# DLRM tower on one core: the order of the step turned, the pairwise products two samples wide, the flattened product in six slots

## The reference, cut to what matters

```
e = stack([tbl_f[ids[:, f]] for f in range(26)])        # 2048 x 26 x 64
x = layer_norm(dense @ Wd.T)                            # 128 per sample
y = layer_norm(e @ Ws.T); y = einsum('bne,pn->bep', y, Wsi); y = layer_norm(y)
T = concatenate([x, y^T])                               # 33 x 128 per sample
Z = T @ T^T; z = layer_norm(Z[lower triangle] @ Wl.T)   # 528 -> 512, 384 kept
h = relu([z, dense] @ W_top1 + b_top1); h = relu(h @ W_top2 + b_top2); out = h @ W_top3
```

## Time and profile before

| | us |
|---|---|
| median of 3 runs | 613.29 |
| the profiled execution | 615.38 |
| its span, first to last instruction | 613.6 |
| PE matmul busy | 529.8 (86%) |
| PE weight loads busy | 376.2 (61%) |
| DVE busy | 435.1 (71%) |
| ACT busy | 259.3 (42%) |
| POOL busy | 395.9 (65%) |
| mean granted TensorE clock | 0.966 |

### The profile page before, as it was taken

How to read it: one execution, slowest core, us unless ns; L and a number is a source line. 1 busy time by engine, 2 the same in 40 slices (tenths; PEclk the granted TensorE clock), 3 DMA queues, 4 the chain that set the end, 5 groups by cost and what they waited for, 6 DMA issues and landing times.

```text
span 613.6 us, 15555 instructions
## 1 busy us (share of the span) xinstructions
PE 529.8 (86%) x6347; PEld 376.2 (61%) x6347; DVE 435.1 (71%) x807; ACT 259.3 (42%) x629; POOL 395.9 (65%) x420
## 2 busy tenths in 40 slices
PE   1466788778789999999999999999999999998877
PEld 1353565465556766666667676767667666755645
DVE  3396689778875797679877886779767976795110
ACT  1113155444343554354544554445544543544212
POOL 5777777777777777777777777777777777200000
PEclk9997789989999999999999999999999999999998
DMA  7911113121212131212222131313121212010100
GB/s 235 366 26 27 27 28 59 36 49 28 58 28 58 29 76 27 57 30 52 50 41 45 30 74 28 59 27 75 30 58 27 58 29 58 13 31 9 24 1 0
DMA packets 28566, 31.65 MB, mean 52 GB/s; under 512 B 9928, under 2 KB 20944, under 8 KB 28112
## 3 DMA queue, kind: packets, MB, share of 16 engines
q0 software_dynamic: 13312, 13.66, 12.4%
q1 hardware_dynamic: 15168, 16.99, 10.5%
q10 hardware_dynamic: 16, 0.01, 0.0%
HBM read 23.28 MB, written 0.01 MB: 38 GB/s over the span
## 4 chain that ended last, share of the span: by engine, by line
PE 54%; POOL 21%; issue 12%; ACT 8%; DVE 4%; DMA 1%; ACTq 0%; SPq 0%
POOL emb L262 21%; PE bank_h L391 11%; PE bank_m L414 10%; PE bank_u L358 8%; PE bank_y L369 5%; PE bank_m L442 5%; PE bank_z L379 4%; PE bank_t L334 3%; ACT zt L627 2%; ACT zbig L578 2%; PE bank_g L344 2%; DVE ssum L831 1%; PE bank_m L449 1%; ACT h L636 1%; ACT embt L551 1%
## 5 line engine op out<-in xcount | busy, mean ns | idle before, releaser
L262 POOL DMA_INDIRECT emb<-in_tables,ids x416 | 395.7, 951 | 130.4 <-issue 122.9
L561 ACT COPY us<-bank_u 128x512 f32<-128x512 f32 x64 | 37.5, 586 | 166.4 <-PE bank_u L358 166.4
L831 DVE TENSOR_REDUCE ssum<-sq 128x32 f32<-128x1024 f32 x64 | 77.8, 1216 | 38.3 <-ACT sq L566 37.2
L391 PE MATMUL bank_h<-wz,zr 128*128 128x512 f32 x224 | 104.0, 594 | 0.6 <-ACT zt L627 0.6
L358 PEld LDWEIGHTS bank_u<-mix_w,emb 128*128 128x128 f32 x512 | 84.8, 204 | 26.9 <-DVE emb L814 15.8
L358 PE MATMUL bank_u<-mix_w,emb 128*128 128x192 f32 (+4 forms) x512 | 89.9, 323 | 11.9 <-DVE emb L814 11.8
L825 DVE TENSOR_TENSOR tt<-bank_y,biasc 128x512 f32<-128x512 f32 x128 | 81.4, 678 | 0.0
L369 PE MATMUL bank_y<-us,proj 64*128 64x512 f32 x256 | 75.8, 666 | 5.4 <-DVE tt L825 5.2
L840 DVE TENSOR_TENSOR tt<-tt,bank_g 128x1024 f32<-128x1024 f32 x64 | 78.1, 1220 | 2.2
L566 ACT ACTIVATE sq<-tt 128x1024 f32<-128x1024 f32 x64 | 68.8, 1075 | 12.6 <-DVE tt L825 12.3
L334 PEld LDWEIGHTS bank_t<-eye,emb 128*128 128x128 f32 x208 | 22.9, 147 | 76.5 <-issue 43.1
(11 more groups left out here) (107 smaller groups left out, 523.4 us busy)
## 6 DMA issues: line engine op xcount, KB each, us to landing
emb<-in_tables,ids POOLq DMA_INDIRECT x416
zs<-zbig SPq DMA_DIRECT2D x64, 70.0 KB
zs<-zbig SPq DMA_DIRECT2D x64, 42.0 KB
dense<-in_dense SPq DMA_DIRECT2D x8, 256.0 KB, 4.5
wfull<-in_wfull SPq DMA_DIRECT2D x1, 2048.0 KB, 10.0
wz<-in_wrows SPq DMA_DIRECT2D x1, 1792.0 KB, 13.6
w<-in_w SPq DMA_DIRECT2D x1, 1280.0 KB
w<-in_w SPq DMA_DIRECT2D x1, 512.0 KB
```

Of the source, the lines that this page charges most:

```text
L262: pool.indirect_dma_start(emb[:, e, t, D * a:D * a + D], None, x_in["tables"], bass.IndirectOffsetOnAxis(ap=ids[:, col:col + 1], axis=0),) ...
L391: mm = pe.matmul(bank_h[:, :], zr[:, s, :], wz[:, s, :], start=(s == 0), stop=(s == SLOTS - 1))
L831: dve.tensor_reduce(ssum[:, h % 2, :], sq[:, :, :], AX.X, ALU.add).then_inc(ssum_ok, 1)
```

## The change

All stages stay and compute the same. What differs:

- The lags shrink (PROD_AT 7 to 3, MOVE_AT 11 to 6, FLAT_AT 13 to 8, top1 22 to 17), STEPS falls from 81 to 76.
- PE's order in a step becomes turn, mix, gram, project, first half of the products, top1 and flat pieces, second half of the products, top3, top2, dense_x, turn_x, sum_x, turn_z, late. ACT and DVE follow.
- Products take two samples at a time: 64 weight columns by 68 moving columns, half of the result unused. A chunk has 16 such matmuls in two rounds of 8. Each round fills 272 columns of bank_z, and the second waits until `products_out` has copied the first. tt, zbig and the DVE and ACT operations on them get a last dimension of two samples.
- `scale_t` keeps its reciprocals in bank_z (before: in bank_g) and so waits for the copies of the chunk in front.
- `flat` has 6 slots in three pieces of 2; the move has 12 DMAs per unit (before 8). In the last unit ACT issues six of them.
- The gathers of a chunk wait for turned and, for a second part, for the first round of products.
- The last super is computed in two halves of 128 samples.

```
-TURN_AT, GRAM_AT, SCALE_AT, MIX_AT, PROJ_AT, CHAIN_AT, PROD_AT, ZOUT_AT = 2, 3, 4, 4, 5, 6, 7, 8
-XCOL_AT, MOVE_AT, FLAT_AT, TURNZ_AT, GAINZ_AT = 6, 11, 13, 16, 17
-TOP1_AT, TOP2_AT, TOP3_AT = (22, 23, 24), 28, 29
+TURN_AT, GRAM_AT, SCALE_AT, MIX_AT, PROJ_AT, CHAIN_AT, PROD_AT, ZOUT_AT = 1, 1, 1, 2, 2, 2, 3, 3
+XCOL_AT, SUMCOL_AT, MOVE_AT, FLAT_AT, TURNZ_AT, GAINZ_AT = 2, 3, 6, 8, 11, 12
+TOP1_AT, TOP2_AT, TOP3_AT = (17, 18, 19), 23, 24
+TAIL = 8 * LAST + 7
-PIECES = ((0, 3), (3, 5), (5, 7))
+PIECES = ((0, 2), (2, 4), (4, 6))
+HALVES = ((0, 2), (2, 4)), ((4, 6), (6, 7)), ((7, 9), (9, 10)), ((10, 12), (12, 13))
+WIDE = 2
+ROUNDS = ((0, 4), (4, 8))
...
# gathers (POOL)
-                    after(pool, grammed, 4 * u + c - 3)
+                    after(pool, turned, 4 * u + c - 2)
+                    for part, (t0, t1) in enumerate(HALVES[c]):
+                        if part == 1:
+                            after(pool, z_done, NR * (4 * u + c - 5) + 1)
...
# the move (SP)
+                for j in range(4 if u < NU - 1 else 2):
+                    for part in range(3):
+                        sp.dma_start(rows_to(j, part), rows_from(u % 2, j, part)).then_inc(zs_in[u % 2], 16)
...
# products (PE)
+            def products(u, h, i):
+                if i == 0:
+                    pe.wait_ge(t_ok, 4 * u + h + 1)
+                    pe.wait_ge(xcol_ok, u + 1)
+                after(pe, zc_ok, NR * (4 * u + h) + i)
+                g0, g1 = ROUNDS[i]
+                for g in range(g0, g1):
+                    for q in range(4 // WIDE):
+                        o = ZC * WIDE * (g - g0)
+                        some = tt[:, u % 2, 4 // WIDE * (8 * h + g) + q, :, :].rearrange("p c w -> p (c w)")
+                        mm = pe.matmul(bank_z[TILE * q:TILE * q + TILE, o:o + ZC * WIDE],
+                                       some[:, C0 * WIDE:ZC * WIDE], some, start=True, stop=True)
...
# the step of ACT, new order
+                c = chunk(s, GRAM_AT)
+                if c:
+                    rows_out(*c)
...
+                if se:
+                    root_e(*se)
+                if pj:
+                    squares(*pj, 0)
+                    squares(*pj, 1)
+                if pd:
+                    products_out(*pd, 0)
+                if pd:
+                    products_out(*pd, 1)
+                if pd == (NU - 1, 3):
+                    move_rest()
+                if pj:
+                    root_s(*pj)
...
# scale_t and the step of DVE, new order
-                after(dve, prod_ok, min(4 * u + h + CHAIN_AT - SCALE_AT + 1, 4 * NU))
-                srs = bank_g[:, 0:2 * GRP]
+                after(dve, zc_ok, NR * (4 * u + h))
+                srs = bank_z[:, 512 - 2 * GRP:512]
...
+                if se:
+                    times_e(*se)
+                    reduce_e(*se)
...
+                if pj:
+                    add_bias(*pj)
+                if se:
+                    scale_e(*se)
+                if pj:
+                    sum_s(*pj)
+                    scale_t(*pj)
```

More of the change, by code:

```diff
@@ L54 @@
 CZ = C0 + ZC
[L55 to L59, removed]
+SLOTS = 6
+SPAN = ((0, 11, 2, 2), (11, 23, 4, 2), (23, 32, 6, 0))
+BASE = (0, 22, 70)
 QS = 8
@@ L130, in top3_of, with col_of, gains_z_of, half_of @@
     return j if j is not None and j < LAST - 1 else None
+def col_of(s, lag):
+    if s == lag:
+        return 0
+    u = unit(s, lag - 1)
+    return u if u else None
+def gains_z_of(s):
+    if s == TAIL + 4:
+        return NU - 2
+    u = unit(s, GAINZ_AT)
+    return u if u is not None and u != NU - 2 else None
+def half_of(s, steps):
+    return steps.index(s) if s in steps else None
 def dlrm(nc, x_in, out):
@@ L370, in project @@
                 mm.then_inc(projected, 1)
[L372 to L378, removed]
-                        mm = pe.matmul(bank_z[PR * j:PR * j + PR, ZC * g:ZC * g + ZC], one[:, C0:ZC], one,
-                                       start=True, stop=True)
+            def products(u, h, i):
[10 more added lines that the diff above has]
+                                       some[:, C0 * WIDE:ZC * WIDE], some, start=True, stop=True)
                 mm.then_inc(z_done, 1)
@@ L534, in _ @@
                     gram(*c)
+                c = chunk(s, PROJ_AT)
+                if c:
+                    project(*c)
+                pd = chunk(s, PROD_AT)
+                if pd:
+                    products(*pd, 0)
+                a = half_of(s, LAST1_AT)
+                if a is not None:
+                    last1(a)
+                if s == TAIL + 5:
+                    open_last()
+                for piece in range(3):
+                    j = top1_of(s, piece)
+                    if j is not None:
+                        top1(j, piece)
+                    u = unit(s, FLAT_AT + piece)
+                    if u is not None:
+                        flat(u, piece)
+                if pd:
+                    products(*pd, 1)
+                j = top3_of(s)
+                if j is not None:
+                    top3(j)
+                j = top2_of(s)
+                if j is not None:
+                    top2(j)
+                a = half_of(s, LAST2_AT)
+                if a is not None:
+                    last2(a)
+                a = half_of(s, LAST3_AT)
+                if a is not None:
+                    last3(a)
+                i = x_of(s, 0)
+                if i is not None:
+                    dense_x(i)
+                i = x_of(s, 1)
+                if i is not None:
+                    turn_x(i)
+                i = x_of(s, 2)
+                if i is not None:
+                    sum_x(i)
+                u = unit(s, TURNZ_AT)
+                if u is not None:
+                    turn_z(u)
                 late(s)
@@ L665, in _ @@
                     mixed_out(*c)
-                c = chunk(s, ZOUT_AT)
-                if c:
-                    products_out(*c)
-                u = unit(s, GAINZ_AT)
-                if u is not None:
+                u = gains_z_of(s)
+                if u is not None and u != NU - 2:
                     gains_z(u)
@@ L876, in _ @@
             for s in range(STEPS):
+                late(s)
                 u = unit(s, TURNZ_AT)
@@ L940 @@
     wrows = wl[np.where(mixed, pair[vec, other], np.where(col == 2, of_x[vec], none))]
-    half = np.where(mixed & ((vec < LOW) == (other < LOW)), 0.5, 1.0).astype(np.float32)
     gq = np.where(mixed, g["L0_rec_gsi"][other], np.float32(1.0))
@@ L985 @@
         "wrows": wrows,
-        "half": half,
         "wx": wx,
```

386 lines of the change are left out of this document (201 added, 185 removed).

## The result

The changed kernel takes **709.37 us**, the median of four runs (705.55 to 710.0), against 614.22 beside it: 1.153 times as long, interval 1.150 to 1.156. The forecast of 608 and the range of 593 to 629 both miss it; the sign is wrong too. The span is 708.2, 100.0 above the forecast's 608.2, and it splits by the same three terms. The starts of the transposes' blocks (PE, one block a step) give them. Steps are counted by their chunk, chunk 16 in step 17; the kernel before transposes it one step of its own later. The lower table averages five cycles, from step 18 on.

The account below looks back on a forecast made before the run. It took POOL's gathers as the ceiling before, and afterwards the loop through PE, DVE and ACT. Step 64 at 544.2 plus tail 64 gave a 608.2 span, 610.0 execution, less 2.1: 608 us, range 593 to 629.

Parts of the forecast that it names:

- the other engines' way from p to p: Loop outside PE between ends of successive steps' second products rounds (p): 6.48 us plus what stands behind the round.
- the second half of the squares 0.55 (half of 1.075): ACT's squares in the other engines' loop: half of the operation takes 0.55 us, half of the earlier 1.075.
- the list of what would show the sum wrong: Signs against the forecast: round far from 0.55, PE waiting for gathers, longer squares or bias adds, lower clock, tail over 70.
- rival A: Main loop: gathers stay the pace at 8.16 us a step; 593 us, to 600 with the tail off; chance 0.24.
- (a): Start of step 17, when the MLP begins: set by chunk 16's 112 gathers, at 147 us.
- the late weights' work: Before step 17: `late` and the half clock at the start could make 147 us into 150.
- (b): The 47 steps from 17 to 64: 8.50 us each, 399.5 less 2.3, so step 64 begins at 544.2.
- twelve moves at 0.64: Moves of products: landed 9.7 us after p (second round's end) of step 2, delaying the gram by 0.5.
- (c): The tail from step 64's start to the end: 64 us, where it was 78.8.
- B: Products rounds cost more, 0.69 us each, and the loop decides: 617 us, or 631 in series; chance 0.30.
- The rule on the tiling mode: PE: changing tiling mode drains TensorE, about 0.2 us left over each time; the two rounds change it twice as often.
- C: The tail does not shrink, through ACT's moves and flat behind the first half: 8 us more, 616; chance 0.08.

Follow-up runs that it names:

- h1: Changed kernel with squares written in reading order and their sum reading at stride two: 670.19 us against 614.60 for the kernel before, 1.091.
- k3: Kernel before, with its squares written and read in the order where each result is 128 bytes from the last: 986.74 us against 978.66 unedited, 1.010.
- h5: Changed kernel with products one sample wide in one round, bank_z copied once; step order, six slots, twelve moves and tail kept: 607.28 us, 0.988 of the kernel before.
- h4: Changed kernel with squares in reading order and the first products copy ahead of the squares on ACT: 661.00 us, 1.074 of the kernel before.
- k1: One-round, one-sample-wide kernel with `z_rows` moved a step later, behind the gram's copy: 827.93 us against 978.66 for the kernel before, 0.848; late instructions.
- k2: Changed kernel with reading-order squares, first copy ahead of them, and `z_rows` a step later: 789.94 us against 978.66 for the kernel before, 0.807; late instructions.
- e5: Changed kernel with products one sample wide in one round, run where instructions are late: 835.73 us, 0.829 of the kernel before.
- e1: Changed kernel with squares in reading order, run where instructions are late: 839.89 us against 1005.31 for the kernel before, 0.840.
- k4: Changed kernel with only `WIDE = 1`, still two rounds of 16 products, where instructions are late: 806.39 us against 978.66 for the kernel before, 0.822.
- h3: Changed kernel with the first products copy ahead of the still slow squares on ACT: 665.66 us, 1.082 of the kernel before.

## Why the prediction was wrong

**The step that failed** is in the other engines' way from p to p: "the second half of the squares 0.55 (half of 1.075)". It measured 1.11, because the profile page's 1075 was taken for a cost of the elements alone while the change turned the order in which they are written. The row was read and halved; the new access pattern of the same line was not looked at. It was in the list of what would show the sum wrong ("squares or the strided bias adds longer than 0.55 and 0.64"); the bias adds were right (two in 1.28). It was no rival, and the range did not hold a loop whose longest link may double. It is the largest single step that failed, 39 of the 95 us by the medians of h1, and not the only one: with the squares cured h1 is still 9.1% slower than the kernel before, and the terms below have the rest.

The Trainium skill speaks of it: SBUF — State Buffer, section Door 1: The DMA port swizzle, says that accesses which stay in one 16-byte line run at full rate and that each crossing to another line pays, "4 fp32" being what one may stride for free. The runs agree, for ScalarE's writes: 128 bytes apart 1108 ns, in order 630; and a read at stride two, two values to such a line, 674. The reads of k3, which jump 136 bytes, add nothing that shows. The size is the runs': 0.93 ns more for each of 512 results.

By 1.11 in place of 0.55 the forecast's way would have been 0.55 longer in the five steps of eight that it set by the sum (rival A says four), 2.8 us in eight; measured are 5.2 (h1 against after). From the end of the bias adds to the copy it is 1.27 against 0.58, 0.69 a step, since the first half too is still running when the second could start: 3.5 us in five steps. Part of the rest is the clock. PE in after, then in h1, at the same place of the cycle:

```profile
397.69 0.69 PE L413 MATMUL bank_z<-tt 128*64 128x68 f32 x16 [3.58 <-ACT zbig L656]
398.32 5.41 PE L507 MATMUL bank_m<-h,w 128*128 128x256 f32 x16
```

```profile
370.44 0.69 PE L413 MATMUL bank_z<-tt 128*64 128x68 f32 x16 [2.87 <-ACT zbig L657]
371.07 3.72 PE L507 MATMUL bank_m<-h,w 128*128 128x256 f32 x16
```

Behind the longer wait the same 16 matmuls of top2 take 1.7 us more, part of them at 1.2 instead of 2.4 GHz: the granted clock is 0.54 from 398.3 to 402.0, and 1.00 in h1's row. In after all six top2 of the loop take 5.3 to 6.3, in h1 three of six take 3.72; the means differ by 1.1.

By the terms of the sum:

- **(a), 30 us.** "Steps without MLP work are shorter than a gather step (7.5), so gathers set it: 147." From step 3 to 17 after makes 10.2 us a step. 12.8 of the 30 are the squares (h1 starts at 164.4). That leaves 17 in h1 and 14 in h5. The gathers are not to blame: the last one of chunk 16 starts at 145.1 us in h5, as before (145.3), but its transposes follow 16.1 us later instead of 2.4. Two waits of PE stand out. One is the late weights' work, which I had put at 3: in after DVE spends 5.48 us on one part of it in the middle of the loop, and PE waits 9.26 us for bank_z (all engines of after, from 40 us); in h5 it waits 7.7 at this place:

```profile
40.11 5.48 DVE L890 SCALAR_TENSOR_TENSOR part<-wfull,bq,part 128x512 f32<-128x512 f32 x7
...
50.52 1.18 PE L413 MATMUL bank_z<-tt 128*64 128x68 f32 x16 [9.26 <-ACT zbig L656]
```

  The other is the moves, on which (a) had nothing: in h5 the grams of steps 8, 12 and 16 wait 5.4, 2.9 and 4.3 us, 12.6 in all, for the copy behind `z_rows`, and the granted clock is 0.50 from 84.2 to 91.0. The first of them:

```profile
86.18 0.83 ACT L661 COPY zr<-zs 128x768 f32<-128x768 f32 x1 [4.13 <-DMA zs<-zbig]
...
87.44 1.65 PE L375 MATMUL bank_g<-gram_w,embt 128*128 128x128 f32 x6 [5.43 <-ACT embt L623]
```

  The kernel before has the late weights' work too, but no wait for the moves, and starts step 17 at 147.8. What each of the two waits costs by itself no run shows.
- **(b), 61.8 us.** Squares 30.1 (h1). h4, without that wait, keeps 23 us over the forecast, 4.2 in eight steps, and the table parts them. *PE's own work* is 66.8, forecast 62.5. The two rounds are 1.25 a step (1.15), the pieces of top1 and flat between them some 0.2 longer than in the sum, and behind four of the six waits of step 0 the clock fell. *The moves:* "twelve moves at 0.64 ... issued 7.0 and landed 9.7 us after p"; they took 0.83 each and were in after 11.9. PE waits 2.0 for them in step 4 in all of the wide kernels, and in h4 2.3 more in step 0, of which the forecast said "At step 7 top2 covers it": 4.3 where it had 0.5. Own work and moves are so 4.3 and 3.8 over the forecast; h4's other waits, 1.1 where the forecast had 5.0, give 3.9 back. That the moves' waits would be won whole if the moves were quicker is argued, not shown: the runs for it (k1, k2) fell where instructions are late.
- **(c), 8.0 us.** Forecast 64, measured 72.0, and 70 to 75 in all of the wide kernels; one-round h5 has 57.6. The missing handover was ACT's six moves between the last round and the relu: I had counted "six moves on each of two queues 3.8", and top2 behind them at full clock. They took 5.1, and top2 6.39 for 3.46. The gain of the short matmuls is real: before had 79.1.

Of the rivals, **A** is refuted: POOL waits for PE 94.4 us. **B** had the right place, the loop, with a wrong link: a round gives way to the next operation after 0.62, not 0.55, against its 0.63 from which it decides; two of them make 1.25 a step where I had 1.15, some 4 us of 100 in 47 steps. The rule on the tiling mode that stood beside it gains a little: the four matmuls of flat hold PE for 1.81 where a round of products follows (h4, steps 1 and 2) and 1.72 where transposes do (h5). **C** is right in kind (8.0 against its 8), and small beside the rest. The loop's own mechanism (PE, DVE and ACT from p to p; PE waiting for bank_z in steps 4 to 7) was seen rightly; the moves and what they hold up were priced too low.

**h5 shows the remaining parts' worth.** The turned order, six slots and twelve moves are 1.2% faster than before once the width and the second round are gone: 21.5 us won in the tail, 13.4 lost at the start, the 47 steps even (387.8 against 386.7).

## What to carry to other kernels

When a change turns the layout of a tensor, price again every operation that writes it: the number of elements is the same, the cost may not be (630 and 1108 ns here), and the trace of before has no row for it. Where a loop goes through several engines, list what each engine's queue has ahead of the link; the cheapest cure here was one line moved (44 of 95 us), not the faster operation. A wait on PE can be paid twice, once in time and once in the clock of what follows. And a wait that a longer one covers comes to light when that one is cured: in after the gram of step 0 never waited for the moves, in h4 it does, 2.3 us each time.

## What the runs showed of the hardware

**Late instructions.** On chips 2, 3, 5, 7 and 12 the kernel before took 977 to 1017 us (medians), on chips 0 and 9 614.6 to 615.7. The single operations last as long, but the idle time before them is put down to the issue or to something not in the trace. PE and its weight loads in the narrow kernel (e5), and the same in k3, the kernel before with slow squares:

```profile
PEld bank_z L413 <- issue: 219.4, 269, 2.4
PE bank_z L413 <- issue: 150.9, 180, 3.0
```

```profile
PEld bank_z L379 <- issue: 150.6, 241, 5.9
...
PE bank_z L379 <- issue: 85.3, 184, 1.8
```

The kernel before has 24.2 us of PEld's wait for issue at bank_z where it takes 614. The losses: before, with 6347 matmuls on PE, 363 to 403 us; the plain squares (e1 against h1), with 4327, 170; the narrow kernel (e5 against h5), with 6375, 228. The count alone does not decide it. k4 has the same 6375, its products in rounds of 32 instead of blocks of 64, and does not wait for them in this way:

```profile
PE bank_z L413 <- issue: 0.5, 1, 0.5
```

The changed kernel itself was not run there. On those chips every kernel that keeps the turned order is ahead (0.81 to 0.85), and the narrow kernel, best where before takes 614, is no better than the wide ones. What makes a chip the one or the other, no run shows.

**Clock.** The granted clock fell from 0.966 (before) to 0.930 (after), and is 0.948 in h1, 0.966 in h3, 0.951 in h4 and 0.958 in h5. It fell where PE had idled, as in after's row of top2 above; not every wait does it (1.00 behind h1's 2.87 us, and from 413 to 416 us behind h4's 1.90).
